# First two token tiles of row 3 routed as sorted pairs with row 2; dense FFN for the other two tiles

## The chip, the cores and the metric

The kernel runs on one core of one Trainium2 chip. The metric is the device time of one execution in microseconds. TensorE is PE in the rows, VectorE DVE, ScalarE ACT, GpSimd POOL and SyncE SP.

## The reference, cut to what matters

Four batch rows of 512 tokens with 256 channels pass one block: a state space mixer and a mixture of eight experts, each behind an adaptive layer norm and a gate. All is float32.

```python
h = _layernorm(x, axis=-1) * (1 + ca) + sa
x = x + ga * _L0_attn_ref(h, ...)          # projection, causal conv, silu, chunked scan, output projection
h = _layernorm(x, axis=-1) * (1 + cb) + sb
x = x + gb * _L0_ffn_ref(h, ...)

# the FFN, for all T = 2048 tokens
logits = jnp.tanh(xt @ Wg1.T) @ Wg2.T                   # 8 experts
_, top_idx = jax.lax.top_k(logits, K)                   # K = 2
top_scores = softmax of the two top logits
scores = jnp.zeros_like(logits).at[rows, top_idx].set(top_scores)
h = silu(jnp.einsum('td,ehd->teh', xt, Wup) + bup)      # 128 hidden per expert
down = jnp.einsum('teh,eoh->teo', h, Wdown) + bdown
out = jnp.einsum('te,teo->to', scores, down)
```

Only two of the eight experts count for a token, so a kernel may compute all eight for it (dense) or only its two (a token then gives two token-expert pairs).

## The kernel before, in words

A tile is 128 tokens; a row has 4 (TPB). `program_order()` writes one list of steps, and each engine walks that list and issues its own part of each step, in order, with semaphores between the engines. SP has a list of its own (`pairs()`, `load_rows`, `load_weights`, `know_rows`, lines 837 to 884). Row by row ("slots" 0 to 3) the list holds for each tile the steps of the scan (tr, bt, state, y), then z (transpose and multiply by the silu gate), out (output projection) and norm. Into the gaps between them the table GAPS puts other work: "p" the next row's input projection, "z" its own, "G" one step of pair work, and named steps of the row before: hid (transpose the normalized rows), gate1, gate2, score, spread, rank (place of each pair among its expert's), scat, bias, plan, plan2.

Rows 0 to 2 go the sorted way. POOL multiplies a normalized tile by its norm's scale (`scaled_row`, into hb) and scatters it twice by indirect DMA (scat) into `pair_rows` in HBM, where each expert has a region. A plan per group (rows 0 and 1 are group 0, row 2 is group 1) counts the tiles of each expert and writes to tab where each of a fixed number of pair tiles begins: 23 for group 0 and 15 for group 1, the worst case. Pair tiles go in quads of four (6 and 4 quads), with three kinds of step: gt transposes a quad's rows, gu is the up matmul of a half quad (a "pair" of two tiles, on SP a weight pair), gd its down matmul. ACT applies silu and stores the results into `pair_out`; the combine step (comb) gathers a tile's two results with two indirect DMAs on POOL, and DVE scales and adds them.

SP reads a quad's row numbers from tab into registers (4 reads), loads its rows and, for each pair tile, the expert's weights (256 KB). Weights go round a ring of 6 tiles, so the load of weight pair n waits for gd of pair n − 3:

```python
if pair >= W_RING // 2:
    wait_bank(sp, ("gd",) + divmod(pair - W_RING // 2, 2))
```

and rows go round a ring of 8, so a quad's rows wait for gt two quads earlier. Row 3 takes the dense way at the end, behind all pair work: up and bc (spread of a score over the 128 hidden rows) for eight experts with 512 tokens each, then down for four tiles. Lines of PE: 1619 hid, 1870 gate1, 1878 gate2, 1750 gt, 1759 gu, 1768 gd, 1850 z, 1859 out, 1904 up, 1911 bc, 1922 down. PSUM has eight banks, one step's output each (`bank_jobs`); pair work in the body uses 7 and 2, which hid, gate1, gate2, bt and rank use too, and a step that finds its bank unread waits (`wait_bank_free`).

## Time and profile before

| | us |
|---|---|
| median of 3 runs | 454.06 |
| lowest, highest | 452.78, 458.48 |
| the profiled execution | 455.36 |
| its span, first to last instruction | 453.1 |
| PE busy in the span | 389.9 (86%) |
| DVE busy | 285.2 (63%) |
| ACT busy | 166.7 (37%) |
| POOL busy | 138.8 (31%) |

The span is what the profile shows; the execution's own time is 2.26 us more. Busy shares are averages over stages with different limits. In "[1.33 <-issue]" the number is the idle time of the engine before that row, and behind the arrow stands what ended it; "issue" is nothing that the profile shows. PEclk is the granted clock of TensorE, 1.00 being 2.4 GHz.

### The profile page before, as it was taken

What the parts mean: (1) busy time and instruction counts of PE and PEld (TensorE: products, weight loads), DVE (VectorE), ACT (ScalarE), POOL (GpSimd) and SP (SyncE); (2) the same over time, 40 slices, a digit from 0 to 9 for tenths busy, and PEclk for the clock granted to TensorE, in tenths of its full rate; (3) what the DMA queues carried; (4) which work ended last, traced back from release to release, by engine and by line L of the source; (5) the groups of instructions that cost most, each with busy time, mean ns of one, the idle gap of its engine ahead of it and who ended that gap; (6) DMA issues with size and microseconds to landing.
All of it is one profiled execution on the core that took longest, in us unless ns stands there. A gap on an engine that the chain in (4) does not pass through costs nothing.

```text
span 453.1 us, 8779 instructions
## 1 busy us (share of the span) xinstructions
PE 389.9 (86%) x3224; PEld 250.1 (55%) x3224; DVE 285.2 (63%) x624; ACT 166.7 (37%) x291; POOL 138.8 (31%) x170
## 2 busy tenths in 40 slices
PE   7799698888878999698998969696979886978997
PEld 4378343455635556356655545463867775664365
DVE  4733648898895558998458987733645531152566
ACT  1516757542423253333343323122432534443310
POOL 1300200423134334042771131653245100715230
PEclk9859799999989999999999899977999998888999
DMA  8999911100000102000321000036367579877123
GB/s 255 368 385 387 377 65 23 60 14 2 3 2 2 52 21 61 1 2 3 109 57 61 0 4 1 25 119 199 86 207 255 173 224 352 282 265 243 47 70 116
DMA packets 45820, 56.41 MB, mean 124 GB/s; under 512 B 4228, under 2 KB 37676, under 8 KB 45764
## 3 DMA queue, kind: packets, MB, share of 16 engines
q1 hardware_dynamic: 38276, 44.38, 30.0%
q0 software_dynamic: 2304, 6.29, 4.3%
q10 hardware_dynamic: 5184, 4.98, 3.2%
q8 instruction: 36, 0.59, 0.6%
q14 instruction: 20, 0.16, 0.1%
HBM read 32.82 MB, written 22.82 MB: 123 GB/s over the span
## 4 chain that ended last, share of the span: by engine, by line
PE 53%; DVE 27%; issue 7%; DMA 4%; ACT 4%; SPq 3%; POOL 1%; DVEq 0%; ACTq 0%; POOLq 0%
PE ps L1703 14%; DVE conv L1315 13%; PE ps L1759 4%; PE ps L1859 4%; PE ps L1904 4%; PE ps L1922 3%; PE ps L1768 3%; PE ps L1782 3%; PE ps L1629 2%; PE ps L1833 2%; PE ps L1663 2%; DMA conv<-pair_rows 2%; PE ps L1750 2%; PE ps L1802 2%; DMA conv<-x 1%
## 5 line engine op out<-in xcount | busy, mean ns | idle before, releaser
L1703 PE MATMUL ps<-hT,win 128*128 128x512 f32 x256 | 134.3, 653 | 9.1 <-DVE conv L1315 7.9
L1315 DVE SCALAR_TENSOR_TENSOR conv<-ps,small,conv 128x511 f32<-128x511 f32 x144 | 106.8, 746 | 33.8 <-ACT conv L1143 30.4
L1703 PEld LDWEIGHTS ps<-hT,win 128*128 128x128 f32 x256 | 47.8, 204 | 54.0 <-issue 38.0
L1143 ACT ACTIVATE conv<-ps,small 128x512 f32<-128x512 f32 x48 | 37.2, 775 | 78.7 <-PE ps L1703 78.7
L947 POOL TENSOR_SCALAR rst<-mv 128x1 f32<-128x1 f32 x16 | 3.6, 225 | 126.5 <-DVE mv L1265 126.5
L1072 ACT ACTIVATE conv<-conv 128x512 f32<-128x512 f32 x48 | 29.7, 624 | 33.1 <-DVE conv L1315 33.0
L1058 POOL DMA_INDIRECT conv<-pair_out,ysloti x24 | 24.1, 1006 | 42.3 <-DVE x L1586 28.3
L1859 PE MATMUL ps<-wog,yT 128*128 128x256 f32 x128 | 31.2, 387 | 1.6 <-issue 1.6
L1859 PEld LDWEIGHTS ps<-wog,yT 128*128 128x128 f32 x128 | 24.2, 195 | 10.8 <-issue 8.2
L1629 PE MATMUL ps<-cst,conv 128*128 128x128 f32 x128 | 20.6, 285 | 10.4 <-ACT conv L1072 4.5
L1629 PEld LDWEIGHTS ps<-cst,conv 128*128 128x128 f32 x128 | 15.1, 145 | 23.6 <-issue 13.8
L1039 POOL DMA_INDIRECT pair_rows<-hs,sloti x24 | 24.3, 1012 | 6.9 <-issue 6.9
L1759 PE MATMUL ps<-conv,hs 128*128 128x128 f32 x152 | 22.8, 301 | 4.1 <-DMA hs<-w_pair 2.8
L1013 POOL TENSOR_TENSOR xv<-xtok,fv 128x512 f32<-128x512 f32 x16 | 17.5, 1096 | 26.9 <-ACT xtok L1199 26.8
L1759 PEld LDWEIGHTS ps<-conv,hs 128*128 128x128 f32 x152 | 20.4, 210 | 6.3 <-issue 4.8
L1802 PEld LDWEIGHTS ps<-xv,btok 64*64 64x64 f32 x448 | 12.9, 140 | 18.6 <-issue 11.2
L1148 ACT ACTIVATE sz<-ps,small 128x512 f32<-128x512 f32 x16 | 10.9, 684 | 32.3 <-PE ps L1703 20.3
L1802 PE MATMUL ps<-xv,btok 64*64 64x64 f32 x448 | 15.1, 231 | 8.0 <-ACT btok L1206 3.3
L1768 PE MATMUL ps<-hs,conv 128*128 128x256 f32 x76 | 19.8, 397 | 0.9 <-DVE hT L1572 0.8
L1833 PE MATMUL ps<-xv,gm 64*64 64x64 f32 x512 | 18.4, 221 | 2.2 <-PE ps L1820 1.0
L1173 ACT ACTIVATE conv<-ps,bupt 128x128 f32<-128x128 f32 x38 | 11.9, 363 | 20.8 <-PE ps L1759 20.8
L1833 PEld LDWEIGHTS ps<-xv,gm 64*64 64x64 f32 x512 | 16.2, 134 | 4.4 <-PE ps L1820 4.4
(189 smaller groups left out, 615.4 us busy)
## 6 DMA issues: line engine op xcount, KB each, us to landing
pair_rows<-zrow SPq DMA_DIRECT2D x1, 12288.0 KB, 43.3
hs<-w_pair SPq DMA_DIRECT2D x38, 256.0 KB, 4.3
conv<-pair_rows SPq DMA_DIRECT2D x38, 128.0 KB, 2.6
pair_out<-conv ACTq DMA_DIRECT2D x18, 256.0 KB, 4.7
conv<-x SPq DMA_DIRECT2D x4, 512.0 KB, 7.7
wog<-w_out_T SPq DMA_DIRECT2D x4, 512.0 KB
win<-w_in_T SPq DMA_DIRECT2D x2, 512.0 KB, 7.8
hs<-w_mod SPq DMA_DIRECT2D x1, 1024.0 KB, 9.6
```

Of the source, the lines that this page charges most:

```text
L1039: pool.indirect_dma_start(xs_d, bass.IndirectOffsetOnAxis(routed(sloti, b, k, i), 0), hb[b][:, i, :], None, bounds_check=N_SLOT - 1, oob_i ...
L1058: pool.indirect_dma_start(yg[:, n % 4, k, :], None, ys_d[g], bass.IndirectOffsetOnAxis(routed(ysloti, b, k, i), 0), bounds_check=GROUP_TIL ...
L1072: act.activation(dst, dst, ACT.Silu).then_inc(silu_done, 1)
L1143: act.activation(conv[:, b % 2, m, :], bank(step), ACT.Identity, bias=cb[:, m:m + 1], scale=cw[:, m, KSIZE - 1:KSIZE]).then_inc(tap0, 1)
L1315: dve.scalar_tensor_tensor(out=dst, in0=bank(("proj", b, m))[:, 0:SEQ - s], scalar=cw[:, m, KSIZE - 1 - s:KSIZE - s], in1=dst, op0=ALU.mul ...
L1629: ins = pe.transpose(bank(job)[:, tile_cols(j)], conv[:, b % 2, base + j, tile_cols(i)], ident)
L1703: ins = pe.matmul(bank(step), win[:, k, m * P:(m + 1) * P], hT[:, k, b * SEQ:(b + 1) * SEQ], start=(k == 0), stop=(k == KD - 1))
L1759: ins = pe.matmul(bank(step)[:, tile_cols(t % 2)], wt[:, t % W_RING, k * P:(k + 1) * P], hg[:, q % 2, k, tile_cols(t % QUAD)], start=(k == ...
L1768: ins = pe.matmul(bank(step)[:, j * DM:(j + 1) * DM], hq[:, q % 2, tile_cols(t % QUAD)], wt[:, t % W_RING, KD * D_EXP:], start=True, stop= ...
L1802: ins = pe.matmul(ps[64 * par:64 * par + 64, bank_of[job], j * CHUNK:(j + 1) * CHUNK], btok[rows, n % 2, g * 64:(g + 1) * 64], xv[rows, n ...
L1833: last = pe.matmul(ps[rows, bank_of[job], j * CHUNK:(j + 1) * CHUNK], gm[rows, n % 2, par, j * CHUNK:(j + 1) * CHUNK], xv[rows, n % 2, g * ...
L1859: ins = pe.matmul(bank(step)[:, 0:DM], yT[:, n % 2, m, :], wog[:, m, :], start=(m == 0), stop=(m == CT_ - 1))
```

## The change: what it does

There are now five units instead of four rows: rows 0, 1 and 2, the first two tiles of row 3 (unit 3), and its last two (unit 4, `DENSE`). Unit 3 is routed like rows 0 to 2 and belongs to group 1 with row 2; only unit 4 is dense.

- Group 1 has 12 × 128 pairs instead of 8 × 128: 19 pair tiles instead of 15, 5 quads instead of 4. Its regions are 768 slots instead of 512, so the zero fill of `pair_rows` writes 14,336 rows instead of 12,288.
- In row 3 the gaps get hid_3, gate1_3, gate2_3, score_3, rank_3, spread_3, scat_3 (four scatters) and a fold of the bias; plan1 and plan2_1 move from tiles 2 and 3 to behind the scan of tile 3, ahead of its z. Two "G" fewer stand in the gaps.
- POOL makes two more scaled rows. Their scale rows (hm_3) and results (hb_3) lie in row 2's part of hT; SP loads hm_3 in `pairs()`.
- SP loads weight pair 11 ahead of the first row numbers of group 1 instead of behind them.
- Up, bc and gate matmuls of unit 4 are 256 tokens wide, and there are two down steps. ACT issues the stores of unit 4's output. There are 14 comb steps instead of 12; five stand ahead of the dense part, three between its experts, six around and behind its down steps.

```diff
-N_SPARSE = 3
+N_SPARSE = 4
+DENSE = 4
+UNIT_ROW = (0, 1, 2, 3, 3)
+UNIT_TILES = ((0, TPB), (0, TPB), (0, TPB), (0, 2), (2, TPB))
+PAIR_TOKENS = 14
...
-GROUPS = ((0, 1), (2,))
-REGION = (1024, 512)
-REGION_BITS = (10, 9)
+GROUPS = ((0, 1), (2, 3))
+REGION = (1024, 768)
...
-         ("G G scat", "bias0 G", "G bias1", "G G plan1", "G plan2_1"),
-         ("G G", "G G", "G G", "G G", "G G G")))
+         ("G G scat", "bias0 G", "G bias1 fold_bdn_3", "G G", "hid_3 G"),
+         ("G gate1_3 G", "gate2_3 G", "score_3 G G", "rank_3 G spread_3", "scat_3 plan1 G G plan2_1")))
...
-        hb = [hb_01[:, 0], hb_01[:, 1], hb_01[:, 0]]
+        hb_3, hm_3 = (hT[:, k, 2 * SEQ:3 * SEQ].rearrange("p (a d) -> p a d", d=DM) for k in range(KD))
+        hb = [hb_01[:, 0], hb_01[:, 1], hb_01[:, 0], hb_3]
+        hm_of = [hm, hm, hm, hm_3]
...
-                    e = nc.s_assert_within((rows[q][t] - FIRST_SLOT[g]) >> REGION_BITS[g], 0, N_EXP - 1,
+                    place = rows[q][t] - FIRST_SLOT[g]
+                    e = nc.s_assert_within(((place >> 8) * 11) >> 5 if g else place >> 10, 0, N_EXP - 1,
...
+                wait_bank(sp, ("gate1", 2))
+                for a, part in enumerate((2, 1)):
+                    spread_row(hm_3[:, a, :], part, BATCH - 1, ld_hm)
                 for q in range(N_QUAD):
+                    if q + 2 == FIRST_QUAD[1]:
+                        load_weights(2 * q + 3)
                     if q + 2 < N_QUAD:
                         know_rows(q + 2)
                         load_rows(q + 2)
                     for h in range(2):
-                        if 2 * q + h + 3 < 2 * N_QUAD:
+                        if 2 * q + h + 3 < 2 * N_QUAD and (h or q + 2 != FIRST_QUAD[1]):
                             load_weights(2 * q + h + 3)
...
-            for i in range(TPB):
-                sp.wait_ge(x2_ready, i + 1)
-                sp.dma_start(outr[BATCH - 1][:, i, :], x1_tile(BATCH - 1, i)).then_inc(stored[1], 16)
...
+                elif kind == "down":
+                    i = step[2]
+                    act.wait_ge(x2_ready, i - UNIT_TILES[DENSE][0] + 1)
+                    act.dma_start(out_d.rearrange("b (i p) d -> b p i d", p=P)[BATCH - 1][:, i, :],
+                                  x1_tile(BATCH - 1, i)).then_inc(stored[1], 16)
...
-                        ins = pe.matmul(bank(step), wup[:, k, e * P:(e + 1) * P], hT[:, k, b * SEQ:(b + 1) * SEQ],
+                        ins = pe.matmul(bank(step)[:, 0:unit_width(b)], wup[:, k, e * P:(e + 1) * P], hT[:, k, unit_cols(b)],
```

DVE's order behind the scan of row 3's last tile, before: the sum of y (1439) is followed at once by the z product (1448) and the row statistics behind the output projection (1457, 1264).

```order
L1439 TENSOR_TENSOR ytok<-ytok,xtok 128x512
L1448 TENSOR_TENSOR yT<-ps,sz 128x512
L1457 TENSOR_TENSOR hT<-ps,hT 128x256
L1264 BN_STATS bns<-hT 128x6
L1265 BN_AGGR mv<-bns 128x2
L1292 TENSOR_SCALAR xn<-hT,mv,rst 128x256
```

The same place now, from the ninth row of the plan on (the sum of y is line 1492 there, eight rows of the plan behind it are not shown; the z product is 1501).

```order
L1600 TENSOR_TENSOR eq<-te,rt 128x152
L1602 TENSOR_TENSOR cmp<-eq,shift 128x152
L1603 TENSOR_REDUCE tsh<-cmp 128x19
L1604 SCALAR_TENSOR_TENSOR te<-rt,tsh 128x19
L1607 TENSOR_SCALAR tab<-te 128x19
L1616 TENSOR_TENSOR cmp<-eq,bup 128x152
L1617 TENSOR_REDUCE bupt<-cmp 128x19
L1619 TENSOR_TENSOR ms<-m,shift 128x96
L1621 TENSOR_REDUCE ysl<-ms 128x12
L1622 TENSOR_TENSOR ysloti<-ysl,slot 128x12
L1501 TENSOR_TENSOR yT<-ps,sz 128x512
L1510 TENSOR_TENSOR hT<-ps,hT 128x256
```

All 18 operations of the plan stand between the sum and the product now.

PE's order from the scan of that tile to the transposes of group 1, before (1759 gu, 1768 gd, 1850 z, 1859 out, 1750 gt, 1619 hid).

```order
L1759 MATMUL ps<-conv,hs 128x128 x8
L1768 MATMUL ps<-hs,conv 128x256 x2
L1850 MATMUL ps<-cst,ytok 128x128 x4
L1768 MATMUL ps<-hs,conv 128x256 x2
L1859 MATMUL ps<-wog,yT 128x256 x4
L1759 MATMUL ps<-conv,hs 128x128 x6
L1768 MATMUL ps<-hs,conv 128x256 x3
L1750 MATMUL ps<-cst,conv 128x128 x8
L1619 MATMUL ps<-cst,xn 128x128 x8
```

And now (1789 plan, 1826 gd, 1808 gt, 1908 z, 1817 gu, 1917 out, 1797 bias).

```order
L1789 MATMUL ps<-macc,onesb 128x8
L1826 MATMUL ps<-hs,conv 128x256 x2
L1808 MATMUL ps<-cst,conv 128x128 x6
L1908 MATMUL ps<-cst,ytok 128x128 x4
L1817 MATMUL ps<-conv,hs 128x128 x4
L1917 MATMUL ps<-wog,yT 128x256 x4
L1817 MATMUL ps<-conv,hs 128x128 x4
L1826 MATMUL ps<-hs,conv 128x256 x4
L1817 MATMUL ps<-conv,hs 128x128 x6
L1797 MATMUL ps<-bdg,sT 128x256 x2
```

Two gu pairs and two gd pairs that stood ahead of the last output projection are down to one gu pair; gd of pair 8 is the first half of the row with x4.

SP's order at the first row numbers of group 1, before: weight pairs 9 and 10 (four tiles, the last two shown), then the reads of tab.

```order
L853 ISA
L853 DMA hs<-w_pair 128x512
L853 ISA
L853 DMA hs<-w_pair 128x512
L837 TENSOR_LOAD tab
L837 ISA x2
```

Now (892 the weights, 875 the reads): the one tile of weight pair 11 stands ahead of the reads.

```order
L892 ISA
L892 DMA hs<-w_pair 128x512
L892 ISA
L892 DMA hs<-w_pair 128x512
L892 ISA
L892 DMA hs<-w_pair 128x512
L875 TENSOR_LOAD tab
L875 ISA x2
```

The third load waits for gd of pair 8, so the reads behind it do too.

## Rows read from the trace of the kernel before

**Rows 1.** Page: the chain by engine, and one DMA issue (KB, us to landing).
```profile
PE 53%; DVE 27%; issue 7%; DMA 4%; ACT 4%; SPq 3%; POOL 1%; DVEq 0%; ACTq 0%; POOLq 0%
...
pair_rows<-zrow SPq DMA_DIRECT2D x1, 12288.0 KB, 43.3
```

**Rows 2.** Windows: stretch, its us, busy PE, PEld, DVE, ACT, POOL, PEclk, DMA share, GB/s.
```profile
360.00:414.60 54.60, 44.32 (x296) 35.13 (x295) 15.86 (x47) 23.53 (x54) 16.31 (x19) 0.89 0.85 274
385.00:390.00 5.00, 5.00 (x14) 2.18 (x12) 0.00 (x0) 1.39 (x4) 3.85 (x4) 0.56 1.09 361
414.60:453.10 38.50, 35.38 (x113) 19.37 (x111) 21.51 (x48) 5.88 (x9) 9.40 (x10) 0.97 0.30 93
```

**Rows 3.** Timeline of PE: start, us, engine, line, operation, count, idle before and releaser.
```profile
382.26 0.92 PE L1750 MATMUL ps<-cst,conv 128*128 128x128 f32 x2 [3.21 <-DMA conv<-pair_rows]
...
387.03 3.06 PE L1870 MATMUL ps<-hT,wg 128*8 128x512 f32 x4
...
412.05 0.68 PE L1759 MATMUL ps<-conv,hs 128*128 128x128 f32 x4 [2.07 <-DMA hs<-w_pair]
412.57 2.04 PE L1768 MATMUL ps<-hs,conv 128*128 128x256 f32 x6
...
419.40 1.98 PE L1904 MATMUL ps<-hT,win 128*128 128x512 f32 x4
...
421.63 1.98 PE L1904 MATMUL ps<-hT,win 128*128 128x512 f32 x4
...
437.71 3.72 PE L1922 MATMUL ps<-win,conv 128*128 128x256 f32 x16
...
441.99 3.72 PE L1922 MATMUL ps<-win,conv 128*128 128x256 f32 x16
```

**Rows 4.** Timeline of SP's queue.
```profile
371.32 2.21 SPq L853 DMA_DIRECT2D hs<-w_pair  x3
373.57 0.60 SPq L882 DMA_DIRECT2D win<-w_up_T  x1
377.07 2.33 SPq L843 DMA_DIRECT2D conv<-pair_rows  x4
...
398.99 9.68 SPq L853 DMA_DIRECT2D hs<-w_pair  x5
```

**Rows 5.** The chain of waits in order of time: start, us, what.
```profile
378.63 5.39 DMA conv<-pair_rows
```

**Rows 6.** Timeline of POOL, one gather; then DMA issues from 420 us, and from 405 to 420.
```profile
386.73 1.01 POOL L1058 DMA_INDIRECT conv<-pair_out,ysloti  x1 [0.30 <-issue]
...
out<-hT SPq DMA_DIRECT2D x8, 128.0 KB, 1.8
...
conv<-pair_out,ysloti POOLq DMA_INDIRECT x8, 2.8
...
pair_out<-conv ACTq DMA_DIRECT2D x1, 128.0 KB, 2.4
```

**Rows 7.** Timeline of DVE: first and last of 13 plan operations; of four combine operations.
```profile
347.91 0.23 DVE L1526 TENSOR_TENSOR cmp<-ps,rt 128x64 f32<-128x64 f32 x1 [1.56 <-PE ps L1731]
...
351.12 0.17 DVE L1551 TENSOR_SCALAR tab<-te 128x15 int32<-128x15 f32 x1
...
446.55 0.35 DVE L1581 TENSOR_SCALAR conv<-conv,s 128x256 f32<-128x256 f32 x1
...
447.91 0.42 DVE L1586 TENSOR_TENSOR hT<-hT,conv 128x256 f32<-128x256 f32 x1
```

**Rows 8.** Timeline of ACT: the store of the last pair output.
```profile
415.37 0.34 ACTq L1186 DMA_DIRECT2D pair_out<-conv  x1
```

**Rows 9.** Timeline of PE in row 3.
```profile
356.17 0.66 PE L1629 MATMUL ps<-cst,conv 128*128 128x128 f32 x4 [0.94 <-ACT conv L1184]
...
369.53 0.72 PE L1759 MATMUL ps<-conv,hs 128*128 128x128 f32 x5 [1.33 <-issue]
```

More of the change, by code:

```diff
@@ L191, in filling @@
             out.append(("bias", slot - 1, int(word[-1])))
+        elif word[-2:] == "_3":
+            out.append((word[:-2], 3))
         else:
@@ L194, in filling, with unit_tiles, unit_width, unit_cols @@
     return out
+def unit_tiles(u):
+    return range(*UNIT_TILES[u])
+def unit_width(u):
+    return P * len(unit_tiles(u))
+def unit_cols(u):
+    lo = UNIT_ROW[u] * SEQ + UNIT_TILES[u][0] * P
+    return slice(lo, lo + unit_width(u))
+def pair_tokens_to(u):
+    return sum(len(unit_tiles(v)) for v in range(u + 1))
 def bank_jobs(step, tail):
@@ L598, in releases @@
                     when["out", b, i] = (x1_ready, n + 1)
-                    when["down", b, i] = (x2_ready, i + 1)
                     for a in range(2):
@@ L603, in releases @@
                         when["y", a, b, i] = (ytok_ready, 2 * n + a + 1)
+            for u in range(DENSE + 1):
+                for k in range(KD):
+                    when["hid", u, k] = (hid_ready, KD * u + k + 1)
+                when["gate1", u] = (th_ready, u + 1)
+                when["gate2", u] = (lg_ready, u + 1)
+                when["sT", u] = (sT_ready, u + 1)
+                when["rk", u] = (slotf_ready, u + 1)
+                for h in range(2):
+                    when["bias", u, h] = (bias_added, 2 * u + h + 1)
+            when["s3", DENSE] = (sT_ready, DENSE + 2)
+            for e in range(N_EXP):
+                when["up", DENSE, e] = (h_ready, e + 1)
+                when["bc", DENSE, e] = (hs_ready, e + 1)
+            for n, i in enumerate(unit_tiles(DENSE)):
+                when["down", DENSE, i] = (x2_ready, n + 1)
             when["rows",] = (rows_made, 1)
@@ L1464, in _ @@
                     b = step[1]
+                    nt = len(unit_tiles(b))
                     dve.wait_ge(lg_ready, b + 1)
-                    for i in range(TPB):
+                    for i in range(nt):
                         ins = dve.max(top[:, i, :], lg[:, i, :])
@@ L1608, in tile_cols, with transpose_norm @@
                 return slice(i * P, (i + 1) * P)
-            def transpose_norm(b, name):
+            def transpose_norm(u, name, row, tiles):
                 first = 0 if name == "hT" else N_TILE
-                for i in range(TPB):
-                    n = first + tile_no(b, i)
+                for i in range(len(tiles)):
+                    n = first + tile_no(row, tiles[i])
                     pe.wait_ge(xn_ready, n + 1)
                     for k in range(KD):
-                        job = (name, b, k)
+                        job = (name, u, k)
                         if i == 0:
@@ L1885, in _ @@
                     wait_bank_free(pe, job)
-                    for i in range(TPB):
+                    for i in range(len(unit_tiles(b))):
                         ins = pe.transpose(bank(job)[0:N_EXP, tile_cols(i)], sc[:, i, :], ident)
```

248 lines of the change are left out of this document (130 added, 118 removed).

## The prediction, made blind

> **What bounds the kernel now.** I read the page first: PE has 53% of the chain that ended last, DMA and SP's queue together 7% [rows 1]. Whole-run shares mix stages, so I went on to windows. The change touches nothing on PE before the second tile of row 3, so only the last 105 us matter, and they fall into two parts at 414.60, where the last pair matmul ends (412.57 + 2.04 in [rows 3]; call this moment E). From 360 to 414.60 PE works 44.3 of 54.6 us while the DMA engines are 85% busy; from 414.60 to the end at 453.10 PE works 35.4 of 38.5 us with the DMA engines at 30% [rows 2]. The first part waits for loads, the second is PE doing the dense FFN.
>
> PE's timeline shows what the first part waits for [rows 3]. The transposes of group 1's second quad got their rows at 382.26 after 3.21 us of nothing; the last weight tile came at 412.05 after 2.07. In the same view one dense expert takes 421.63 − 419.40 = 2.23 us and one dense output tile 441.99 − 437.71 = 4.28. SP's timeline [rows 4] shows why loads are late: SP works its list in order, and may load a weight pair only when the down matmul three pairs earlier is through. Between the w_up load at 373.57 and the row loads at 377.07 lie 3.5 us: 0.6 the load, the rest the four register reads that say where a quad's rows are, 2.85 with their gaps. The four row loads take 2.33 on the list, 1.9 to the start of the last and its own issue, and that last one landed 5.39 us after it [rows 5].
>
> **The change, part by part.** Four terms; three move E, one shortens what follows it.
>
> *D, the time after E.* Dense work halves: 8 × 2.23 / 2 = 8.9 us less for the experts, two output tiles or 8.6 us less. If PE still decided, the end would be E + 38.5 − 17.5 = E + 21.0. But the sorted pairs of group 1 now serve six token tiles instead of four, and their gathers may start only when the group's last output is stored. That chain: copy and start of the last store 0.8 us (store issued at 415.37 [rows 8]), its landing 2.4; 12 gathers on POOL, each starting 1.3 us after the one before (1.01 and 0.30 idle), so 11 × 1.3 = 14.3 to the start of the last; its landing 2.8 [rows 6]; four vector operations, 446.55 to 448.33, 1.8 [rows 7]; issue and landing of the output 0.4 + 1.8 [rows 6]. That is 24.3 us, longer than 21.0: **the gathers take the place of the dense FFN as what ends last.** D = 24.3 − 38.5 = −14.2 us.
>
> *A, row 3.* Routing of the first two tiles of row 3 moves in between the scan steps. (a) PE work. Gate 1 for 256 tokens is at most half of 3.06 us [rows 3], 1.0 at full clock; the transposes, gate 2, ranks and score transposes I estimate at 1.4 together. 2.4 us. (b) The last output projection now stands ahead of the down matmul of pair 8, which it followed: 2.2 us, with the transposes that feed it. (c) New hand-overs through PSUM banks 2 and 7, which pair work uses too: the pair matmul behind the hidden transposes, the down matmul behind gate 1, the B transposes behind that, the down matmul behind the ranks, the score transposes behind that. Such a hand-over shows as 0.94 us of idle PE before the transposes at 356.17 [rows 9]. Between nothing (covered by a neighbour) and 5 × 0.94 = 4.7 us I take 4.0, since little work stands between them. (d) DVE: the plan of group 1 (13 operations) and plan2 (5) used to stand between earlier steps; now they stand ahead of the last z product, which the last output projection waits for. The 13 took 347.91 to 351.29, 3.4 us [rows 7]; with 19 tiles instead of 15 in some, and five more of the kind, the 18 take 5.1. PE has one pair matmul of 0.9 us to put in, so with the hand-over it stands 4.6. (e) Gone: 1.33 us at 369.53 [rows 9] and one hand-over of 0.9 behind the plan's matmul. A = 2.4 + 2.2 + 4.0 + 4.6 − 2.2 = 11.0 us. The down matmul of pair 8, which released SP's load at 371.32 [rows 4], then ends near 382.2.
>
> *B, SP's list.* Before, the rows of group 1's first quad were asked for before pair 8 was through. Now SP first loads the last weight tile of group 0, which waits for pair 8, and only then reads the registers and asks for those rows: 2.85 + 1.9 = 4.75 us of issuing ahead of the next weights, the w_up load and the second quad's reads. The tables (ready about 376 by A) are no longer what SP waits for, nor are the four new scatters. 1.05 us of it is hidden, because the next weight pair had to wait for its own down matmul (three loads took 2.21 us, issuing alone some 1.2 [rows 4]). B = +3.7 us, and the second quad's last rows land at 384.0 + 11.0 + 3.7 = 398.7.
>
> *C, from there to E.* Gate 1 leaves this part (3.06 us at 387.03 [rows 3]; half of it now comes before those rows) and gate 2 halves: −3.5. A fifth quad comes in. Near the end a quad costs one round of the weight ring: issue 0.45, landing 3.7 (from the start of the last issue at 408.34, [rows 4], to 412.05, [rows 3]), then up and down matmuls, together 5.4 with what overlaps. C = +1.9 us.
>
> *Costed at nothing.* The zero fill of the scatter buffer grows by a sixth, 7.2 us by its row of 43.3 [rows 1]; what SP issues behind it is first used by the output projection of row 0, behind all that row's projections. Without that cover it is a rival below. Two more broadcast loads on SP lie under the first quad's transposes, for which the next row loads wait; uncovered they cost under 1 us. Two more scaled rows on POOL fall into its waits for VectorE and a third address operation on SP for each weight load of group 1 into its waits for down matmuls; bare, either is below 2 us in all.
>
> **Sum:** 11.0 + 3.7 + 1.9 − 14.2 = **+2.4 us**. The profiled execution took 455.36 us for its span of 453.1, 1.3 above the median of the runs, 454.06. I put the difference on the median: **456.5 us**. A measurement of this kernel tells about 2%, 9 us, from no change; this is none.
>
> The 5.39 us is a landing in a stretch with the DMA engines 85% busy [rows 2, 5]. The Trainium skill ("DMA: Bandwidth & Descriptors", "Anatomy of one DMA — SWDGE (gpsimd) path") gives a DMA a fixed 2.0 us plus its bytes over 436 GB/s, as an estimate 2.3 for such a tile; by it the sum would be −0.7 us instead of +2.4. The gathers' 2.8 us in the quiet end [rows 6] comes near it, the loaded stretch does not, so the measurement decides.
>
> **Rivals.**
> 1. *The idle time absorbs it (faster).* PE idles over 10 us between 360 and 414.60 [rows 2]. If hand-overs, plan and SP's reads fall into idle time that is there anyway, E moves only by the added pair work, under 1.1 us for each of four tiles (by two of the 256-wide and four of the 128-wide passes), less 0.5 for gate 2: E at 418.5, end at 442.8, about 444 us. For it: the slack. Against it: SP's row loads hang on pair 8 in the new list, and pair 8 on the last output projection. Chance 0.17.
> 2. *The half clock (slower).* From 385 to 390, behind the wait of 3.21 us, the granted clock was 0.56 [rows 2]. The change makes longer waits: 4.6 us in row 3 and about 8 before the second quad. From there to E some 11 us of PE work lie on the chain through SP, for each down matmul releases a weight load, which releases the next matmul. At the lower level, 1.2 GHz, that is 11 us more, 9 beyond the sum: 465.5 us. It decides if the clock before E stays near 0.56; at 0.85 it is 2 us and within C. Chance 0.20. The Trainium skill ("TensorE: Matmul & The Clock Gate", "HAM oscillation — how this bites in real kernels") describes short groups of matmuls that each start cold behind a wait for DMA. The trace agrees for 385 to 390, but its 0.89 over the whole part [rows 2] doesn't bear it out for every group.
> 3. *The fill is not covered.* 7.2 us on top: 463.7. Chance 0.03.
> 4. *The gathers start sooner, and the dense path ends last after all:* −3.3 us, 453.2. Chance 0.10.
>
> My forecast has 0.50. Its own range, with C between 0.2 (short rounds) and 4.4 (the half clock in two of them), A ± 3 and B ± 1: 451 to 461.
>
> **How the numbers follow.** Forecast, fourth rival and a third of the third lie within 2%: 0.61. Faster by over 2% is below 445: 0.17. Slower by over 2% is above 463.1: the second rival and most of the third, 0.22. A range for 8 in 10 takes in both outer cases to their middle: 444 to 467.
>
> **What would show it.** A: PE idle for 4 to 5 us before the last output projection (line 1917), released by DVE's product, and the weight load behind pair 8 near 382. B: the row loads of quad 6 (line 881) right behind that, those of quad 7 near 391. C: the last down matmul (line 1826) near 431. D: 12 gathers back to back on POOL from about E + 3.2, DVE's last operation about 22 us after E, the dense matmuls done before. I am wrong if the 12 gathers have gaps, if quad 6's rows are asked for before 378, or if the clock before E is far from 0.85 to 0.9.

## The result, and the profile after

The changed kernel took **481.67 us** (median of 4 runs, 475.18 to 493.82) against 456.27 (4 runs of the kernel before on the same chip, 452.78 to 461.17): a ratio of **1.050, 95% interval 1.029 to 1.071**. The forecast was 456.5 with a range to 467. Executions of one kernel fall into a faster and a slower state, and the ratio compares the faster ones alone (480.38 and 475.18 of the changed kernel), so it is below 481.67 / 456.27 = 1.056. The profiled execution took 482.96 us for a span of 481.0.

Three moments cut the last part of both traces into the same pieces: the start of the second and of the last output projection of row 3 (344.63 and 391.39 after the change, 343.21 and 372.38 before), the end of the last pair matmul (the prediction's E: 452.60 and 414.60), and the end. The windows of the two kernels (stretch, its us, busy PE, PEld, DVE, ACT, POOL, granted clock, DMA share, GB/s), the kernel before:

```profile
343.21:372.38 29.17, 25.05 (x305) 21.75 (x304) 14.57 (x39) 10.97 (x25) 6.14 (x9) 1.00 0.69 224
372.38:414.60 42.22, 33.43 (x176) 25.70 (x176) 11.66 (x37) 18.99 (x43) 15.52 (x17) 0.86 0.88 292
```

The changed kernel, where the last line answers to the last of [rows 2]:

```profile
344.63:391.39 46.76, 34.61 (x305) 26.95 (x305) 19.06 (x65) 12.62 (x29) 10.90 (x14) 0.78 0.40 130
391.39:452.60 61.21, 43.89 (x215) 35.43 (x216) 13.17 (x40) 22.17 (x54) 16.94 (x18) 0.83 0.78 254
452.60:481.00 28.40, 18.29 (x76) 12.39 (x75) 18.95 (x48) 4.16 (x10) 12.67 (x12) 0.91 0.41 125
```

Each stretch can be split into PE's work at full clock (busy time times the mean clock), what the lower clock adds (busy time less that) and PE idle. Change against before, in us:

| stretch | work | clock | idle | sum |
|---|---|---|---|---|
| up to the second output projection | | | | +1.4 |
| row 3, to its last output projection | +2.0 | +7.6 | +8.0 | +17.6 |
| from there to E | +7.7 | +2.8 | +8.5 | +19.0 |
| after E | −17.7 | +0.6 | +7.0 | −10.1 |
| all | −8.0 | +11.0 | +23.5 | +27.9 |

The change does take 8 us of work off PE, and pays for them with 23.5 us of standing and 11 of low clock. The split is rough, since the mean clock of a stretch also counts the time in which PE stands. In row 3 the half clock lay in two places:

```profile
383.47:386.88 3.41, 3.41 (x27) 2.83 (x24) 2.25 (x7) 0.49 (x1) 0.00 (x0) 0.50 0.12 46
356.16:373.23 17.07, 15.92 (x93) 11.61 (x92) 5.29 (x21) 4.71 (x11) 2.15 (x2) 0.50 0.39 116
```

By these PE was busy for 19.33 us at half clock, which costs 9.7 us and not 7.6, and its work in row 3 hardly changed (305 matmul records before and after). A second profile of the changed kernel (e1 below, span 479.4) has 40.7, 63.6 and 28.5 us in the three pieces, so the loss isn't that of one execution. The +1.4 us up to the second output projection of row 3 are no cost of the change: it starts between 342.48 and 350.78 in the sixteen profiles of this document, whatever the kernel.

PE's timeline of row 3 shows both the standing and the low clock:

```profile
353.75 1.16 PE L1817 MATMUL ps<-conv,hs 128*128 128x128 f32 x8 [1.06 <-ACT hT L1259]
355.71 0.68 PE L1686 MATMUL ps<-cst,conv 128*128 128x128 f32 x4 [0.81 <-ACT conv L1216]
...
357.87 2.07 PE L1826 MATMUL ps<-hs,conv 128*128 128x256 f32 x4
...
376.97 1.13 PE L1826 MATMUL ps<-hs,conv 128*128 128x256 f32 x4 [1.21 <-DVE slf L1568]
...
382.84 1.48 PE L1891 MATMUL ps<-xv,gm 64*64 64x64 f32 x32 [2.95 <-remote]
...
391.39 1.97 PE L1917 MATMUL ps<-wog,yT 128*128 128x256 f32 x8 [2.73 <-issue]
```

Four down matmuls of one shape take 2.07 us at 357.87 and 1.13 at 376.97: the first stand in the stretch at half clock. The 2.73 us are the wait for the z product; DVE had 18 plan operations ahead of it, first and last of them here, with the product (compare [rows 7]):

```profile
385.88 0.22 DVE L1582 TENSOR_TENSOR cmp<-ps,rt 128x64 f32<-128x64 f32 x1
...
390.49 0.17 DVE L1622 TENSOR_TENSOR ysloti<-ysl,slot 128x12 uint32<-128x12 f32 x1
390.60 0.69 DVE L1501 TENSOR_TENSOR yT<-ps,sz 128x512 f32<-128x512 f32 x1
```

The 2.95 us end on nothing that the profile names ("remote"): the matmuls at 382.84 (L1891) wait for PE's own previous group alone, which ended at 379.88; before, they followed after 0.17. The granted clock from 355 to 375, before and after:

```profile
355.00:375.00 20.00, 17.57 (x180) 15.49 (x179) 6.97 (x16) 8.04 (x19) 1.28 (x3) 1.00 0.77 234
```
```profile
355.00:375.00 20.00, 18.14 (x106) 13.67 (x107) 5.29 (x21) 6.17 (x15) 2.15 (x2) 0.57 0.37 111
```

106 matmul records in 18.14 us against 180 in 17.57. Behind row 3, SP's list, answering to [rows 4], and PE at the first, the second and the last rows of group 1 (compare [rows 3]):

```profile
386.55 9.09 SPq L892 DMA_DIRECT2D hs<-w_pair  x3
398.51 1.38 SPq L881 DMA_DIRECT2D conv<-pair_rows  x3
...
404.51 2.24 SPq L881 DMA_DIRECT2D conv<-pair_rows  x4
```
```profile
410.99 2.31 PE L1808 MATMUL ps<-cst,conv 128*128 128x128 f32 x8 [5.51 <-DMA conv<-pair_rows]
...
440.29 2.08 PE L1826 MATMUL ps<-hs,conv 128*128 128x256 f32 x4 [4.69 <-issue]
...
451.14 1.46 PE L1826 MATMUL ps<-hs,conv 128*128 128x256 f32 x6
```

The 4.69 us of PE at 440.29 come from ACT, whose silu PE waits for, and ACT itself stood on nothing that the profile names:

```profile
439.61 0.62 ACT L1216 ACTIVATE conv<-ps,bupt 128x128 f32<-128x128 f32 x2 [5.20 <-remote]
```

Stands of ACT like this, of 3 to 5 us, are in all eleven profiles that have the routing in row 3, between 428 and 448, and stands of 3.4 to 3.6 in those of e5, e6 and e7 between 396 and 406. The one profile of the kernel before has none from 340 on, so a comparison with it overstates the loss somewhat.

After E, the first and the last gather on POOL, DVE at the last dense tile and its last operation:

```profile
457.11 0.99 POOL L1101 DMA_INDIRECT conv<-pair_out,ysloti  x1 [17.53 <-DMA pair_out<-conv]
...
472.13 1.00 POOL L1101 DMA_INDIRECT conv<-pair_out,ysloti  x1 [0.30 <-issue]
...
474.57 0.42 DVE L1656 TENSOR_TENSOR scr<-ps,gates 128x256 f32<-128x256 f32 x1 [2.81 <-remote]
...
478.43 0.43 DVE L1642 TENSOR_TENSOR hT<-hT,conv 128x256 f32<-128x256 f32 x1
```

The dense tile that DVE takes up at 474.57 was ready when PE's last matmul ended, at 471.72. These 2.81 us, too, end on nothing that the profile names.

### The profile page after: what moved, and what is told of

Same layout as the page of the kernel before. It is cut to its first block, busy times and chain, and to the rows that moved or that the text cites. A ratio compares the mean times of both kernels' runs of the same rounds, so it can differ in the third digit from the quotient of the medians.

```text
span 481.0 us, 8917 instructions
## 1 busy us (share of the span) xinstructions
PE 392.1 (82%) x3229; PEld 258.9 (54%) x3229; DVE 288.4 (60%) x649; ACT 169.1 (35%) x305; POOL 150.2 (31%) x183
## 3 DMA queue, kind: packets, MB, share of 16 engines
q1 hardware_dynamic: 41476, 48.05, 30.7%
## 4 chain that ended last, share of the span: by engine, by line
PE 47%; DVE 25%; issue 10%; DMA 5%; ACT 4%; another core or an unknown queue 3%; SPq 3%; POOL 1%; DVEq 0%; ACTq 0%; POOLq 0%
PE ps L1760 15%; DVE conv L1368 11%; PE ps L1817 4%; PE ps L1826 4%; PE ps L1917 4%; PE ps L1840 3%; PE ps L1891 2%; PE ps L1686 2%; PE ps L1808 2%; DMA conv<-pair_rows 2%; DMA pair_out<-conv 2%; PE ps L1860 2%; SPq L875 2%; PE ps L1720 1%
## 5 line engine op out<-in xcount | busy, mean ns | idle before, releaser
L1101 POOL DMA_INDIRECT conv<-pair_out,ysloti x28 | 28.8, 1029 | 48.8 <-DMA pair_out<-conv 34.1
L1115 ACT ACTIVATE conv<-conv 128x512 f32<-128x512 f32 x48 | 29.7, 623 | 31.5 <-DVE conv L1368 31.5
L1826 PE MATMUL ps<-hs,conv 128*128 128x256 f32 x84 | 29.3, 494 | 10.1 <-issue 5.7
L1817 PE MATMUL ps<-conv,hs 128*128 128x128 f32 x168 | 26.4, 309 | 5.1 <-DMA hs<-w_pair 2.6
L1686 PE MATMUL ps<-cst,conv 128*128 128x128 f32 x128 | 21.0, 288 | 10.5 <-ACT conv L1115 4.5
L1817 PEld LDWEIGHTS ps<-conv,hs 128*128 128x128 f32 x168 | 23.9, 219 | 7.2 <-issue 2.5
L1826 PEld LDWEIGHTS ps<-hs,conv 128*128 128x128 f32 x84 | 18.5, 239 | 15.5 <-issue 6.6
L1227 ACT ACTIVATE conv<-ps 128x512 f32<-128x512 f32 (+1 forms) x22 | 12.7, 578 | 39.7 <-PE ps L1826 24.7
L1891 PE MATMUL ps<-xv,gm 64*64 64x64 f32 x512 | 19.5, 230 | 6.7 <-remote 4.8
L1056 POOL TENSOR_TENSOR xv<-xtok,fv 128x512 f32<-128x512 f32 x16 | 17.6, 1098 | 22.4 <-ACT xtok L1242 22.3
L1860 PEld LDWEIGHTS ps<-xv,btok 64*64 64x64 f32 x448 | 13.9, 149 | 19.3 <-issue 12.0
L1808 PE MATMUL ps<-cst,conv 128*128 128x128 f32 x84 | 17.6, 358 | 7.8 <-DMA conv<-pair_rows 6.4
```

The source lines that it names most:

```text
L1101: pool.indirect_dma_start(yg[:, n % 4, k, :], None, ys_d[g], bass.IndirectOffsetOnAxis(routed(ysloti, b, k, i), 0), bounds_check=GROUP_TIL ...
L1115: act.activation(dst, dst, ACT.Silu).then_inc(silu_done, 1)
L1686: ins = pe.transpose(bank(job)[:, tile_cols(j)], conv[:, b % 2, base + j, tile_cols(i)], ident)
L1808: ins = pe.transpose(bank(job)[:, tile_cols(t % QUAD)], xg[:, t % RING, k * P:(k + 1) * P], ident)
L1817: ins = pe.matmul(bank(step)[:, tile_cols(t % 2)], wt[:, t % W_RING, k * P:(k + 1) * P], hg[:, q % 2, k, tile_cols(t % QUAD)], start=(k == ...
L1826: ins = pe.matmul(bank(step)[:, j * DM:(j + 1) * DM], hq[:, q % 2, tile_cols(t % QUAD)], wt[:, t % W_RING, KD * D_EXP:], start=True, stop= ...
```

## The experiments

All fourteen in one table, with the three stretches of each profile as above. The medians are over all executions. Single runs of the changed kernel spread widely, and their granted clock goes with them. Its eight runs have these clocks and spans: 0.920 473.1, 0.908 478.3, 0.904 479.4, 0.902 481.0, 0.894 488.6, 0.889 487.4, 0.879 494.6, 0.876 491.9. A straight line through them falls 4.9 us for each 0.01 of clock (correlation −0.97). The last column is the mean distance of a variant's four spans from that line: a comparison at equal clock, rough to some 3 us (outside 0.876 to 0.920 the line is extended).

The ratios on record for changed kernels (e4, e9, e11 to e14) are 1.044 to 1.049, and all lie inside the interval of the changed kernel itself, 1.029 to 1.071. None is on record for e1, e2, e3, e8 and e10. So the times alone tell none of these variants from the changed kernel; what they show stands in their profiles, one of each, and roughly in the last column.

| kernel | median (range) | before, same chip | row 3 | to E | after E | off the line |
|---|---|---|---|---|---|---|
| before | 456.27 | | 29.2 | 42.2 | 38.5 | |
| changed | 481.67 (475.2–493.8) | 456.27 | 46.8 | 61.2 | 28.4 | −1 |
| e1 the same again | 489.89 (481.2–496.7) | 460.48 | 40.7 | 63.6 | 28.5 | +1 |
| e2 filler in row 3 | 484.12 (475.2–485.9) | 460.48 | 42.0 | 62.9 | 28.0 | +2 |
| e3 filler behind row 3 | 490.80 (481.4–497.1) | 460.48 | 49.5 | 63.4 | 29.1 | +8 |
| e4 plan behind z | 481.61 (478.0–486.4) | 460.48 | 47.8 | 59.5 | 28.3 | −2 |
| e5 before, half the dense part | 446.96 (444.8–454.7) | 460.07 | 30.4 | 39.0 | 30.7 | |
| e6 before, fifth quad | 469.91 (467.0–473.3) | 460.07 | 31.7 | 52.6 | 37.4 | |
| e7 before, larger fill | 458.87 (455.7–467.4) | 460.07 | 31.7 | 38.5 | 37.4 | |
| e8 two combines less | 475.47 (465.0–480.1) | 460.07 | 47.7 | 60.2 | 22.9 | −4 |
| e9 routing behind row 3 | 476.31 (475.3–477.7) | 455.43 | 26.6 | 75.1 | 27.9 | −5 |
| e10 SP's order back | 478.03 (466.9–483.3) | 455.43 | 49.5 | 54.7 | 28.2 | −7 |
| e11 four quads | 475.56 (470.8–483.2) | 455.43 | 39.6 | 52.1 | 29.7 | −10 |
| e12 dense tile first | 484.45 (471.6–494.3) | 455.43 | 49.4 | 62.1 | 31.0 | +3 |
| e13 scatter later | 484.74 (481.0–485.7) | 460.84 | 45.8 | 61.6 | 28.3 | −3 |
| e14 e13 and e10 | 483.29 (479.2–486.2) | 460.84 | 49.1 | 59.9 | 28.7 | −3 |

**e1, the changed kernel once more**, with no edit.

> The changed kernel once more, unchanged, so that later edits have a second trace beside them. Theory 1 (half clock): the stretch from the second to the last tile of row 3 runs again at a granted clock well under 1 (0.50 to 0.68 in the first trace), and the time is 473 to 494 us. Rival (single stalls of 3 to 5 us that no engine's signal ends): these sit in other places in this trace, and the clock in row 3 is near 1.

489.89, so the program as it is gives medians 8 us apart. The trace has the half clock at another place: 0.93 up to the third output projection of row 3, 0.72 behind it. The stall of PE is there again, 2.98 us at the same matmuls.

```profile
355.00:375.00 20.00, 15.13 (x145) 11.41 (x149) 7.65 (x32) 7.37 (x19) 4.13 (x6) 0.97 0.36 108
```

With the clock up, the piece from the second to the third output projection of row 3 took 22.3 us instead of 29.2, with the same 201 matmul records.

**e2, e3, filler matmuls.** At the hand-overs of row 3 (e2), or at the waits behind it (e3), PE multiplies bf16 zeros into a free bank. The edit of e2:

```
-         ("G G scat", "bias0 G", "G bias1 fold_bdn_3", "G G", "hid_3 G"),
-         ("G gate1_3 G", "gate2_3 G", "score_3 G G", "rank_3 G spread_3", "scat_3 plan1 G G plan2_1")))
+         ("G G scat", "bias0 G", "G bias1 fold_bdn_3", "G w5x6 G", "hid_3 w3x8 G w3x6"),
+         ("G gate1_3 w3x3 G w3x5", "gate2_3 G", "score_3 G G", "rank_3 w4x8 G w4x6 spread_3", "scat_3 plan1 G G plan2_1")))
```

> Changed kernel with filler matmuls (bf16, 256 wide, into a free PSUM bank, results unused) before the steps of row 3 at which PE waits for a hand-over: 6 + 8 + 6 in tile 2, 3 + 5 + 8 + 6 in tile 3, 16 ahead of the last output projection, 6 us of filler in all at full clock. Theory 1 (the hand-over waits cost mostly by letting the clock fall): clock near 1 from 355 to 375 and 6 to 10 us less in spite of the added work. Rival (the waits cost by their own length alone): same time within 3 us, or some us more.

> Changed kernel with filler matmuls only in the pair work behind row 3, before the steps at which PE waits for rows or weights (40, 6, 6, 12, 6, 6, 16, 8). Theory 1: the clock of 0.5 to 0.66 in parts of 400 to 445 rises, and the end comes 4 to 7 us sooner. Rival (that part hangs on SP's issuing and on landings): within 3 us.

Neither shows a gain. e2 has the clock of its first theory, 0.96 from 355 to 375, but e1 and e11 have 0.97 and 1.00 there without filler. Its 484.12 lies between the 481.67 and the 489.89 of the changed kernel, not the 6 to 10 us lower that were expected. e3 raises the clock from 400 to 450 to 0.92 (0.80 and 0.82 in the changed kernel and e1), and the piece to E takes 63.4 us all the same. Its +8 in the last column says little, since the filler itself raises the mean clock. So filler was not shown to give anything back here.

**e4, the plan of group 1 behind the last z transposes.**

```
-         ... "rank_3 G spread_3", "scat_3 plan1 G G plan2_1")))
+         ... "rank_3 G spread_3", "scat_3 G G")))
-    steps += [("z", b, i), *take(pair_work), ("out", b, i), ...
+    steps += [("z", b, i), ("plan", 1), *take(pair_work), ("plan2", 1), ("out", b, i), ...
```

> Changed kernel with the plan of group 1 and its second part behind the last z product instead of ahead of it. My forecast (PE stands 4.6 us for it): 2.5 to 4.5 us less; the wait before the last output projection goes, and SP's first row numbers still wait for the down matmul of pair 8, now sooner. Rival (the plan's tables become the wait of SP's list): no gain, SP's first read of group 1 stands behind the tables.

Ratio 1.048 (1.036 to 1.060). The wait of 2.73 us ahead of the last output projection is gone from its trace, another of 0.91 stands one step earlier, and the half clock took the rest: the last tile of row 3 needs 18.0 us instead of 17.6, at a clock of 0.75 instead of 0.90 and with 5.9 us idle instead of 7.7. Step (d) was read rightly, and taking its wait away gave nothing that the times show.

**e5, e6, e7, the three other parts of the change, each alone on the kernel before.** e5 does the dense part for the last two tiles of row 3 only, at half width (the FFN of the first two is left out), with the last combines around its two down steps. e6 plans group 1 with 19 tiles, so that five quads run:

```
 GROUP_TILES = tuple((PICKS * len(rows) * SEQ + N_EXP * (P - 1)) // P for rows in GROUPS)
+GROUP_TILES = (23, 19)
```

e7 fills as much as the changed kernel:

```
-N_SLOT = N_EXP * sum(REGION)
+N_SLOT = N_EXP * (sum(REGION) + 256)
```

> Kernel before with the dense FFN computed for the last two tiles of row 3 only; the FFN of its first two tiles is left out. No routing of them, no added pairs. All theories: about 17 us less (8.9 for the experts, 8.6 for two output tiles), if the gathers of row 2 stay hidden (E + 19 by my chain against E + 21): 434 to 440 us. This is the most that the change could bring. If the gain is far smaller, the gathers or the stores already set the end, and term D fails.

> Kernel before with 19 pair tiles and 5 quads planned for group 1 instead of 15 and 4 (the added tiles hold no pairs). No routing, dense FFN whole. My term C without the gate part: one more round of the ring, 5.4 us, 4 to 8 with the clock; E moves by that, and so does the end. Rival for the missing 8 us of C (a longer pair part loses to the clock or to DMA): 10 us or more.

> Kernel before with 14,336 rows zero filled instead of 12,288. Forecast: no change, within 1%. Rival 3 of the prediction: 7 us more.

e5: ratio 0.974 (0.964 to 0.984), 12 us less. e6: 1.022 (1.013 to 1.030), 10 us more. e7: 1.004 (0.998 to 1.010): the fill is covered, as costed. The trade itself, half the dense part for a fifth quad, so gives 2 us by the middle values, before any routing is paid. The two intervals make that an estimate of 2 ± 6, so its sign isn't shown, and the four gathers of unit 3 aren't in it. e5 gained 12 us where 17 were expected: behind E it needs 30.7 us, not 21. There PE waited 3.12 us for DVE and ran one of the two down steps at half clock (6.50 us against 3.72). Its last gather started at 430.20, 9 us ahead of DVE's end, so the gathers aren't what ended it. e6 came out near the 10 us of its rival, not at 5.4. Its piece from row 3 to E has 40.02 × 0.87 = 34.8 us of work against 28.7 before, 6.1 more, and 12.5 us idle against 8.8:

```profile
381.17:433.73 52.56, 40.02 (x208) 32.12 (x208) 11.67 (x37) 22.01 (x51) 16.95 (x18) 0.87 0.87 285
```

In e7, which does the work of the kernel before, the same piece took 38.5 us instead of 42.2: a piece of a single profile is good to some 4 us.

**e8, the changed kernel without the last two combines.**

```
-                    for k in range(PICKS):
+                    for k in range(PICKS if b < 3 else 0):
```

> Changed kernel without the last two combine steps (four gathers; the FFN of the first two tiles of row 3 is left out of the output). If the gathers end last, as term D has it, 4 to 5.5 us less, and the dense path then decides. Rival (dense path or stores end last): no change.

After E 22.9 us instead of 28.4, 5.5 less, and the dense path then ends last: DVE takes up the last dense tile at 471.77, right behind PE.

```profile
471.77 0.42 DVE L1660 TENSOR_TENSOR scr<-ps,gates 128x256 f32<-128x256 f32 x1
```

But the 5.5 us aren't the price of four gathers. In the changed kernel DVE stood 2.81 us ahead of that tile, and two combines of some 1.7 us each came behind it; e8 has neither. The gathers as such, whose last would have landed near 474.9 (472.13 and the 2.8 of [rows 6]), were not waited for in that profile. So e8 doesn't show that the gathers end last.

**e9, the routing of unit 3 behind row 3.**

```
-         ("G G scat", "bias0 G", "G bias1 fold_bdn_3", "G G", "hid_3 G"),
-         ("G gate1_3 G", "gate2_3 G", "score_3 G G", "rank_3 G spread_3", "scat_3 plan1 G G plan2_1")))
+         ("G G scat", "bias0 G", "G bias1 fold_bdn_3", "G G", "G"),
+         ("G G", "G", "G G", "G", "G")))
...
+              ("hid", 3), *take(pair_work, 2), ("gate1", 3), *take(pair_work), ("gate2", 3), *take(pair_work), ("score", 3),
+              *take(pair_work), ("rank", 3), *take(pair_work), ("spread", 3), ("scat", 3), ("plan", 1), ("plan2", 1),
```

> The changed kernel with the routing of unit 3 (hidden transposes, both gates, scores, ranks, scatter, plan of group 1) moved out of the gaps of row 3's scan to behind the last output projection; the same number of pair steps in row 3's gaps. Theory one (the hand-overs and the low clock they bring into row 3 are the cost): the two stretches from the second to the fourth output projection of row 3, 29.2 and 17.6 us in the changed kernel, fall to about 21 and 11, as in the kernels that leave row 3 alone; the routing chain, 12 to 15 us of steps that wait for one another, then stands behind the last output projection and is covered for some 9 us by pair work; the time falls by 8 to 12, to about 473. Theory two (the added steps cost the same wherever they stand): within 3 us of the changed kernel, 479 to 485.

The first half of the expectation holds beyond its number: row 3 takes 26.6 us, 20 less than changed and 2.6 less than before, at full clock from 355 to 375 where the changed kernel had 0.57. It has 21 pair steps in the gaps of row 3, the changed kernel 22 and the kernel before 25: one fewer than the changed kernel, not the same number, and the change took out three "G", not two. A pair step is worth about 1 us of PE.

```profile
355.00:375.00 20.00, 18.35 (x206) 15.43 (x204) 6.89 (x16) 7.59 (x17) 3.62 (x6) 1.00 0.57 179
```

But the chain that was hidden in row 3 now stands bare, and gives back 14 of the 20: PE waits 9.89 and 5.16 us for the first two quads of group 1, and the half clock comes there.

```profile
397.36 0.45 PE L1810 MATMUL ps<-cst,conv 128*128 128x128 f32 x1 [9.89 <-DMA conv<-pair_rows]
...
406.91 2.51 PE L1810 MATMUL ps<-cst,conv 128*128 128x128 f32 x8 [5.16 <-DMA conv<-pair_rows]
```
```profile
385.00:405.00 20.00, 4.72 (x17) 3.09 (x17) 5.09 (x21) 2.59 (x5) 12.11 (x12) 0.56 0.61 204
```

476.31 is 5.4 below 481.67, half of what was expected, and 21 above the kernel before. But the ratio, 1.049 (1.041 to 1.057), is that of the changed kernel, so the gain in time isn't shown; what is shown is where the time stands.

**e10, SP's order as before.**

```
-                    if q + 2 == FIRST_QUAD[1]:
-                        load_weights(2 * q + 3)
...
-                        if 2 * q + h + 3 < 2 * N_QUAD and (h or q + 2 != FIRST_QUAD[1]):
+                        if 2 * q + h + 3 < 2 * N_QUAD:
```

> The changed kernel with SP's list as before: the weights of pair 11 are asked for behind the first row numbers of group 1, not ahead of them. The prediction's step B (4.0 us in the trace of the changed kernel): the second quad's rows land 3 to 4 us sooner and the time falls by as much, to about 478. Rival: SP now waits for the tables of group 1 with the weights of pair 11 behind it, so that the last pair of group 0 comes late by the same amount: no change, 480 to 484.

From row 3 to E 54.7 us instead of 61.2, 6.5 less (4.9 of it idle time, at a clock of 0.88 instead of 0.83); the rows of the second quad are waited for in three pieces of 0.26, 0.77 and 0.39 instead of one of 5.51. Step B was right in its mechanism. Its own profile doesn't show the gain as a whole, since its row 3 took 49.5 us.

```profile
412.55 0.33 PE L1806 MATMUL ps<-cst,conv 128*128 128x128 f32 x1 [0.77 <-DMA conv<-pair_rows]
```

**e11, the changed kernel with four quads in group 1.**

```
+GROUP_TILES = (23, 15)
 GROUP_QUADS = tuple(-(-n // QUAD) for n in GROUP_TILES)
```

> The changed kernel with group 1 cut to 15 tiles in four quads, as before the change; the pairs that belong in the last four tiles are left out of the computation. If a quad costs what the kernel before showed when one was added (about 10 us): 470 to 472. If it costs the 5.4 us of the prediction's step C: 476. If its cost lies in waits for the first quads of group 1 and not in its own work: over 478.

Ratio 1.047 (1.031 to 1.063); 9.1 us less to E, 10 at equal clock. That agrees with e6 from the other side: a quad costs 9 to 10 us. The median by itself, 475.56, can't tell the case of 10 us from that of 5.4: it is 6 below the first four runs of the changed kernel and 11 below the median of all eight.

**e12, both dense tiles ahead of the last five combines.**

```
-    steps += [("bc", d, N_EXP - 1), *take(combs, 2)]
+    steps += [("bc", d, N_EXP - 1)]
     for i in range(*UNIT_TILES[d]):
-        steps += [("down", d, i), *take(combs, 2)]
+        steps += [("down", d, i), *take(combs)]
+    steps += take(combs, len(combs))
```

> The changed kernel with the dense output tile of the last token tile put ahead of the last six combines instead of between them. In its trace the vector engine waited 2.81 us for that tile with the last two combines behind it. If that wait is on the path: 1.5 to 3 us less, 479 to 480. If the last gathers, which land about as late, end the kernel anyway: no change.

No gain (31.0 us after E, 2.6 more). Its gathers now wait for free buffers, which DVE hands back later, for 3.27 and 1.97 us:

```profile
479.67 1.00 POOL L1102 DMA_INDIRECT conv<-pair_out,ysloti  x1 [3.27 <-DVE hT L1643]
...
483.95 1.00 POOL L1102 DMA_INDIRECT conv<-pair_out,ysloti  x1 [1.97 <-DVE hT L1643]
```

**e13, the scatters of unit 3 held back on POOL; e14, that and e10 together.**

```
                     pool.wait_ge(hb_ready, pair_tokens_to(b))
+                    if b == 3:
+                        pool.wait_ge(ysum_ready, N_TILE)
```

> The changed kernel with the four scatters of unit 3 held back on POOL until the vector engine has summed y of row 3's last tile. If the stall of 2.8 to 3.0 us of PE ahead of the last within-chunk products comes from the scatters that POOL issues at that moment: it is gone or down to the 0.17 us of the other tiles, and the stretch from the third to the fourth output projection of row 3 falls from 17.6 to 14.7. If it has to do with where PE's own instructions come from: the stall stays at 2.8 to 3.0. Either way the rows land some 7 us later, which the wait for the weights of pair 11 on SP's list covers.

> As e13, and SP's list as before the change, as in e10. In e10 the stretch from the last output projection to the last pair matmul was 54.7 us against 59.5 to 63.6 in the kernels with the changed list. If the gains add: that stretch about 55 us and the one before it 14.7, the time near 473 and still above the kernel before by 15 or more. If the later scatters now hold back the first rows of group 1, for which SP no longer has the weights of pair 11 to cover them: that stretch is 57 to 60 and the time as in the changed kernel, 480.

In both, the stall ahead of the last within-chunk products is gone, and the last tile of row 3 takes 15.1 and 15.2 us instead of 17.6. The row of e13:

```profile
385.56 1.15 PE L1893 MATMUL ps<-xv,gm 64*64 64x64 f32 x32 [0.17 <-PE ps L1880]
...
389.67 0.48 PE L1828 MATMUL ps<-hs,conv 128*128 128x256 f32 x1 [2.09 <-issue]
```

A new stop of 2.09 us (2.11 in e14) stands 2 us further on. And the gains don't add: in e14 the later scatters hold back SP, PE waits 5.38 us for the weights of pair 11, and the piece to E is 59.9 us, as the second case of its expectation said. Ratios 1.047 (1.038 to 1.057) and 1.044 (1.034 to 1.053).

## Why the prediction was wrong

Its four terms against the trace of the changed kernel:

| term | predicted | measured | what was missed |
|---|---|---|---|
| A, row 3 to the down matmul of pair 8 | +11.0 | +24.0 | half clock 8 to 10, stall 2.95, a start 1.4 later |
| B, SP's list | +3.7 | +3.7 | nothing |
| C, from there to E | +1.9 | +10.3 | a quad at 9 to 10 instead of 5.4, clock 2.8 |
| D, after E | −14.2 | −10.1 | start and spacing of the gathers, a stand of DVE |
| sum | +2.4 | +27.9 | |

Of the 25.5 us by which the sum was off, A has 13.0, C 8.4 and D 4.1. A is measured at SP's load behind pair 8 (395.31 against 371.32), B at the start of the last row load of the second quad (406.29 against 378.63), C from there to E.

**A failed first: it had no term for the clock.** Its waits were read nearly rightly: (c), (d) and (e) together made 6.4 us of idle time, the trace has 8.0, of which 2.95 is the stall that no row before showed. The stall is no accident: it is 2.81 to 2.98 us in all nine profiles that have unit 3's scatters at that place. What (a) to (e) left out is that row 3, with these waits of about 1 us between short groups of matmuls, runs in part at half clock. In the profiles of the kernel before and of e5, e6 and e7 the clock from 355 to 375 was 1.00. With the routing in the gaps it was 0.57 in the changed kernel and 0.50 to 0.53 over 360 to 380 in e10 and e13; with the same routing moved out (e9) 1.00. It isn't certain in each execution: e1 had 0.97 and e11 1.00 there. Nor is row 3 free of it without the routing, since e6 and e7 had 0.66 from 335 to 355. Over the whole of row 3 the low clock cost 1.1 to 13.1 us in the eleven profiles with the routing in the gaps and 0 to 2.5 in the five without, by the split above; idle time was 5.8 to 12.2 us against 2.6 to 4.1. In e11 the piece from the second to the third output projection took 22.4 us, against 29.2: so the added work and hand-overs are worth 4 us there (before 18.2), and the half clock 7.

Rival 2 had the right mechanism and the wrong place. It put the half clock between row 3 and E, where the clock was 0.83 against 0.86, and gave it 9 us and a chance of 0.20; the whole last part shows 11. Even that rival, at 465.5, is 16 us short of the median. Over all runs the line of the section above, extended, gives 468 us for the changed kernel at a mean clock of 0.93, where the 35 runs of the kernel before with a clock on record have 457. By it about 11 of some 28 us are the changed order's own and about 17 go with the lower clock; the pair of profiles says 11 for the clock and 17 for the rest. The two don't agree, since a run with longer waits has both the longer time and the lower clock, and the line gives the clock all of it. No run holds the clock fixed; e2 and e3, which tried to, failed. e9 shows that the half clock goes where the routing goes; which of its steps bring it is not shown.

The Trainium skill ("TensorE: Matmul & The Clock Gate", "HAM oscillation — how this bites in real kernels") describes short groups of matmuls that each start cold behind a wait. The trace of row 3 agrees in part: the half clock came at 356.16 behind waits of 1.06 and 0.81 us, on ACT and not on DMA, but it then stayed for 17.07 us in which PE was busy for 15.92. The prediction weighed that rule only for the part between row 3 and E.

**B held.** The rows of the first quad were asked for right behind the weights of pair 11, at 398.51, and e10 took the step back for 6.5 us of that piece. The −0.7 us that the prediction works out with 2.3 in place of the landing of 5.39 is wrong: that landing stands in the kernel before as well as after, so it is no term of the sum.

**C was a term sized by the wrong row.** The prediction priced the fifth quad by one round of the weight ring, 5.4 us. A quad is four pair tiles with two such rounds: e6 shows 6.1 us of work at full clock and 3.7 of added idle time. Some of the rest is the 4.69 us in which PE waited for the standing ACT. Rival 1 erred the same way, in part: it priced a tile at 1.1 us and let all waiting be absorbed. The trace of the changed kernel speaks against absorption anywhere, since idle time grew by 23.5 us.

**D had the right row of gathers, and its end was another.** The gathers run in an unbroken row, as forecast. The first came at E + 4.5 instead of 3.2; eleven spacings took 15.0 instead of 14.3; and from the start of the last gather to DVE's end lie 6.7 us instead of 4.6. These 6.7 don't hang on the last landing, but on DVE's stand of 2.81 us ahead of the last dense tile, with two combines still open behind it. Such a stand, 2.2 to 2.8 us, is in six profiles of changed kernels. With no stand DVE would have come to the last combine before its rows landed, and the forecast 4.6 would have held, by an estimate from these rows (474.9 and 1.8 of combine are 476.7). e12 shows that the other order isn't to be had for nothing. Rival 4 had the gathers start sooner, and they started later. Rival 3 falls with e7.

The range of the forecast itself was summed wrongly: with C up by 2.5, A by 3 and B by 1 it ends at 463 and not at 461, and D had no allowance at all. The measured 481.67 is outside either.

The signs named beforehand: PE did stand ahead of the last output projection, for 2.73 us instead of 4 to 5, behind DVE; the weights behind pair 8 came at 395 instead of 382, the last down matmul ended at 452.6 instead of 431, and DVE's last operation 26 us after E instead of 22. "If the clock before E is far from 0.85 to 0.9" was watched in the wrong stretch.

**What stays open.** What the 2.95 us are. In four profiles a packet of 16 KB on the queue that the profile calls q8 instruction moved 0.8 to 1.4 us before PE went on (at 382.0 in the changed kernel, 377.2 in e1, 386.4 in e4, 383.0 in e8), and POOL's scatters kept the DMA engines busy in that moment. The slice from 382.0 to 382.2 of the changed kernel (packets, MB, share of 16 engines):

```profile
q0 software_dynamic: 20, 0.07, 80.6%
q8 instruction: 1, 0.02, 27.5%
```

With the scatters later (e13) that packet moved at 387.2, and a stop of 2.09 us followed, from 387.58 on. The first scatter there started at 388.96, so the scatters can't be the whole cause of a stop. The kernel before has such a packet at 366.6, in row 3's last tile too, and there PE went on and stood for only 1.33 us, ending at 369.53 [rows 9]. That PE waits for its own instructions there fits most of this and is not shown; nor is what ACT and DVE stood for. Nor is it shown why one execution takes the half clock in row 3 and another does not. No version that computes the whole block beats the kernel before. The best pieces (row 3 of e9, SP's list of e10) can't simply be joined: e9's chain would need pair work that row 3 has already used. This is argued; no run tried it.

## What to carry to other kernels

Price an added block by its whole group in the trace, all its matmuls and all its rounds, and not by the one wait that it makes visible: the fifth quad cost 9 to 10 us, the round 5.4. When steps that hand over from engine to engine are threaded into a dense stretch of PE, ask what the granted clock of that stretch is worth before asking about the waits: 8 us of waits in row 3 came with 8 to 10 us of half clock, where the stretch had run at 1.00. Take more than one profile of each kernel before reading pieces of 3 to 4 us: the same work differed by that much. And before moving a chain out of a dense stretch, look for what will cover it at its new place: e9 won 20 us in row 3 and gave back 14.

## What the runs showed of the hardware that was not expected

- One program, run eight times, had spans of 473.1 to 494.6 us, with mean granted clocks of 0.920 down to 0.879 beside them (and 0.876 at 491.9). The kernel before, with fewer short waits, had spans of 449.7 to 468.0 at clocks from 0.947 down to 0.912 in 35 runs.
- A stretch of 20 us with PE busy for 18.14 can still be at half clock (0.57): the busy share says nothing of it, since slower matmuls fill the time. The count of matmul records does: 106 against 180.
- PE, ACT and DVE each stood at times for 2 to 5 us on nothing in the profile (PE 2.95 at 382.84, ACT 5.20 at 439.61, DVE 2.81 at 474.57). PE's came back at the same matmuls in nine profiles (2.81 to 2.98), and a shorter one, 2.09, stood 2 us further on when POOL's scatters were held back.
- Indirect gathers on POOL followed each other every 1.4 us (eleven spacings in 15.0); 2 MB more of zero fill under other work gave nothing measurable, 1.004 (0.998 to 1.010).
